# Attention and routed experts on one core: row statistics taken one batch ahead, and the order of the hand-over changed

## The chip, the cores and the metric

One core of a Trainium2 chip runs the whole program. The metric is device time in microseconds (us), lower is better. A run is one execution; the kernel before has three plain ones and one that was profiled.

## The reference

The input `x` is 8 batches of 512 rows of 512 values. Cut to what matters:

```python
xn = (x - mean(x)) / sqrt(var(x) + 1e-5)              # per row
qkv = xn @ Wqkv.T + b_qkv                             # 16 heads of 32
p = softmax(q @ k.T / sqrt(32) + alibi_bias, causal)
s = (p @ v).reshape(...) @ Wout.T + b_out
top_idx = argmax(softmax(xn @ w_router.T))            # 2 experts
h = xn @ w_fc[top].T; a = where(h >= 0, h, 0.5 * h) ** 2
g = silu((a @ w_proj[top].T) * top_weight)
out = x + s * g
```

## The kernel before

The core's engines run programs of their own, written out by hand, each in its own order, and wait for one another on semaphores: TensorE (PE), VectorE (DVE), ScalarE (ACT), GpSimd (POOL), and SyncE (SP), which issues most DMAs.

**Attention** runs batch by batch. `batches` calls each engine's `iteration(b, odd)` for b from -1 to 8; an iteration has 16 steps, one for each head. In one step TensorE transposes the probabilities of this head (L446, `ptrans`), works one or two jobs of the table `JOBS`, and makes the scores of the head four steps ahead (L425, `scores`). The jobs of a step are in `STEP`:

```python
JOBS = [("q", 0, 2), ("ctx", -1, 3), ("k", 0, 2), ("q", 0, 3), ("k", 0, 3),
        ("o", -1, 0), ("x", 1, 0), ("ctx", 0, 0), ("o", -1, 1), ("x", 1, 1),
        ("x", 1, 2), ("o", -1, 2), ("o", -1, 3), ("x", 1, 3),
        ("q", 1, 0), ("ctx", 0, 1), ("logits", 1, 0), ("k", 1, 0), ("q", 1, 1),
        ("k", 1, 1), ("v", 1, 0), ("ctx", 0, 2), ("rank", 1, 0), ("v", 1, 1),
        ("v", 1, 2), ("v", 1, 3)]
STEP = [(0, 1), (2,), (3,), (4,), (5, 6, 7), (8, 9), (10, 11), (12, 13),
        (14, 15), (16, 17), (18,), (19,), (20, 21), (23, 22), (24,), (25,)]
```

The second entry of a job is the batch it belongs to, counted from b, and the third its part. So steps 0 to 3 make the last q and k of batch b, steps 4 to 7 its predecessor's output projection and the transposes of xn for batch b+1, steps 8 to 15 q, k, router logits, v and ranks of batch b+1. "ctx" (L461, `pv`) is the product of probabilities and v for four heads.

VectorE works through one step in this order: `rden` (L868, the reciprocal of the softmax sums of the next head); four masked row minima (L857, `masked`) for the head three steps ahead; `read_out` of the step's job, which for q and k is the cast to 16 bits L782 of what ScalarE has staged (L519); the copy of a third of the transposes (L844, `turned`); then what the step has besides. That is, before the change: `ln_stats` (L749, L750: mean and variance of the rows of batch b+1) twice each in steps 0 and 1, `ln_apply` (L756) in steps 2 to 5, the largest weight (L888) in four steps, and the cast `cx` of a finished context (L900).

TensorE's last score of a step waits for the fourth `masked` of that step (`ttr_done`). Its transposes in step n+1 wait for GpSimd's normalisation `pr` (L941, four instructions) that GpSimd runs in step n, after `rden`. GpSimd also makes the low halves `pre` (L947) and `cx` (L961), the reciprocal deviations `veps` and `rstd` (L953, L956) in step 1, and the indirect DMAs that write each row's routing record (`route`, L969) in steps 14 and 15. `choose` (L784, in step 9) picks the expert from the logits, `place` (L802, in step 13) works out where each row goes.

**Hand-over and experts.** In the last attention batch (b = 7) and in iteration 8 the program finds the scales of the expert weights (`weight_row`, `weight_scales`), splits the first six pieces of them into two 16-bit halves (`split_hi` on ScalarE L1163, `split_lo` on VectorE L1225), and transposes the first rows of the experts (`xtrans` L1080, `turn_hi` L1174, `turn_lo` L1249). Iteration 8 also reads out the last context (L528, L900, L961), for which the last output projection waits (L352, x48). Then come 17 slots of 256 rows through the experts (L1106, L1126).

## Time and profile before

| | |
|---|---|
| median of three runs | 1480.56 us (1479.88 to 1480.98) |
| the profiled execution, its own time | 1481.51 us |
| its span, first to last instruction | 1479.7 us |
| mean granted TensorE clock | 0.987 of full speed |
| busy share of the span: PE, DVE, ACT, POOL | 94%, 62%, 52%, 46% |
| one full attention batch (of which six run alike) | about 85.4 us |
| start of the expert part | about 755.5 us |

The span and the time of a run differ by 1.8 us, which lies outside the first and the last instruction. Step 0 of the batch looked at most starts at 235.1 us and the next batch at 320.6 us. In the timelines below, the first number is the start in us from the span's start, the second how long the entry took (x4: four instructions together), and brackets at the end give how long the engine had stood idle just before and what ended that. A busy time of TensorE counts overlapping matmuls, so its gaps are better read from starts.

### The profile page before, as it was taken

The numbers are of one execution on the slowest core, as the hardware profiler recorded it, in microseconds if no ns is written. First come the engines' busy times: TensorE is split into PE (matmuls) and PEld (weight loads), VectorE is DVE, ScalarE is ACT, GpSimd is POOL, SyncE is SP. The second block draws the span as 40 slices with busy tenths as digits, with TensorE's granted clock in tenths as the row PEclk, the third lists the DMA queues.
The fourth block names the chain that finished last, engine by engine and source line by source line (L and its number), as shares of the span: only waits on it lengthen the run. The fifth ranks groups of instructions, "written<-read, shape, count | busy, mean of one in ns | idle before, by whom it ended". The sixth has DMA issues, their size and how long they took to land.

```text
span 1479.7 us, 30039 instructions
## 1 busy us (share of the span) xinstructions
PE 1384.0 (94%) x9863; PEld 880.8 (60%) x9863; DVE 923.9 (62%) x2441; ACT 770.7 (52%) x1824; POOL 682.5 (46%) x896
## 2 busy tenths in 40 slices
PE   2889999999999999999689999999999999999995
PEld 1455555655555565555456666666666666666663
DVE  7577777777777777777759745555444555544444
ACT  3478778787777878787736422222222222222221
POOL 0356667465666746566523433333333333323332
...
GB/s 161 144 86 148 125 115 125 110 139 100 171 101 130 128 106 138 89 141 140 107 164 207 115 44 44 44 43 25 23 41 42 39 44 44 30 29 30 36 30 30
DMA packets 84897, 133.45 MB, mean 90 GB/s; under 512 B 14095, under 2 KB 63247, under 8 KB 82576
## 3 DMA queue, kind: packets, MB, share of 16 engines
...
## 4 chain that ended last, share of the span: by engine, by line
PE 75%; DVE 10%; POOL 6%; ACT 3%; issue 3%; DMA 1%; DVEq 1%; SPq 0%; ACTq 0%; POOLq 0%
PE psY L1126 19%; PE psF L1106 19%; PE psA L352 19%; PE psT L446 7%; PE psA L461 5%; POOL pr L941 4%; PE psS L425 3%; DVE sg L1303 2%; PE psX L1080 1%; POOL route L969 1%; PE psA L409 1%; DVE stat L749 1%; DVE am L636 1%; ACT stage L519 1%; DVE wf L1225 1%
## 5 line engine op out<-in xcount | busy, mean ns | idle before, releaser
L1106 PE MATMUL psF<-xT,wf 128*128 128x256 f16 (+1 forms) x3264 | 368.0, 269 | 0.0
L1126 PE MATMUL psY<-wf,aT 128*128 x1584 | 363.9, 379 | 0.3 <-DVE aT L1270 0.3
L1106 PEld LDWEIGHTS psF<-xT,wf 128*128 x3264 | 312.0, 98 | 63.5
L1344 POOL TENSOR_TENSOR a<-a 128x512 f32<-128x512 f32 (+1 forms) x136 | 153.1, 1126 | 392.1 <-DVE a L1261 390.5
L941 POOL TENSOR_SCALAR pr<-pr,rden 128x128 f32<-128x128 f32 (+3 forms) x512 | 268.4, 542 | 141.9 <-DVE rden L868 140.3
L579 ACT ACTIVATE pr<-pr,mn 128x128 f32<-128x128 f32 (+3 forms) x512 | 281.9, 553 | 0.0
L857 DVE CUSTOM_DVE_ANT_0 pr<-psS,base,nsl 128x128 f32<-128x128 f32 (+3 forms) x512 | 249.6, 543 | 4.2 <-PE psS L425 4.2
L1126 PEld LDWEIGHTS psY<-wf,aT 128*128 128x128 f16 x1584 | 154.5, 98 | 158.5 <-issue 1.0
L446 PE MATMUL psT<-conf,pr 128*128 128x128 f32 x1280 | 205.7, 279 | 18.1 <-POOL pr L941 16.5
L1183 ACT ACTIVATE rl<-psF 128x512 f32<-128x512 f32 (+1 forms) x136 | 79.3, 583 | 263.2 <-PE psF L1106 263.0
L446 PEld LDWEIGHTS psT<-conf,pr 128*128 128x128 f32 x1280 | 157.3, 143 | 81.3 <-POOL pr L941 27.3
L1190 ACT ACTIVATE aT<-a 128x512 f16<-128x512 f32 (+1 forms) x136 | 84.0, 618 | 230.9 <-POOL a L1344 230.9
L352 PE MATMUL psA<-xT,wqkv 128*128 128x512 f16 x768 | 188.8, 386 | 14.4 <-DVE wqkv L667 13.1
L1261 DVE SCALAR_TENSOR_TENSOR a<-psF,rl 128x512 f32<-128x512 f32 (+1 forms) x136 | 91.7, 674 | 169.4 <-ACT rl L1183 168.5
L566 ACT ACTIVATE pt<-psT 128x512 f32<-128x512 f32 x256 | 151.6, 593 | 62.0 <-PE psT L446 56.2
L1270 DVE TENSOR_TENSOR aT<-a,aT 128x512 f16<-128x512 f32 (+1 forms) x136 | 91.3, 672 | 128.9 <-ACT aT L1190 116.1
L352 PEld LDWEIGHTS psA<-xT,wqkv 128*128 128x128 f16 x768 | 74.9, 99 | 83.8 <-DVE wqkv L667 13.5
L947 POOL TENSOR_TENSOR pre<-stage,pre 128x512 f16<-128x512 f32 x64 | 74.1, 1158 | 90.3 <-DVE pre L782 90.3
L425 PE MATMUL psS<-ks,qs 128*128 128x128 f16 (+3 forms) x512 | 99.8, 304 | 16.2 <-DVE mn L857 12.7
L352 PE MATMUL psA<-wout,cx 128*128 128x512 f16 x384 | 93.2, 385 | 7.4 <-POOL cx L961 7.4
L579 ACT ACTIVATION_READ_ACCUMULATOR pr<-pr,mn 128x1 f32 x512 | 98.3, 192 | 0.0
L782 DVE CAST pre<-stage 128x512 f16<-128x512 f32 x64 | 34.1, 532 | 100.4 <-ACT stage L519 97.8
...
## 6 DMA issues: line engine op xcount, KB each, us to landing
...
qs<-qk_parts SPq DMA_DIRECT2D x128, 128.0 KB, 2.7
ks<-qk_parts SPq DMA_DIRECT2D x128, 128.0 KB, 2.7
...
```

What stands on the lines that cost most here:

```text
L352: last = nc.tensor.matmul(ps, a, x, start=(n == 0), stop=(n == len(pairs) - 1))
L425: nc.tensor.matmul(rows[i], qs[:, par, j, i * P:(i + 1) * P], ks[:, par, j, 0:(i + 1) * P], start=True, stop=True).then_inc(s["S_done"], 1)
L446: last = nc.tensor.transpose(ps[:, o:o + P], pr[:, j, c:c + P], conf[:, C_ID:C_ID + P])
L566: nc.scalar.activation(pt[:, g % 2, j, o:o + w], psT[r][:, 0:w], ACT.Copy).then_inc(s["T_act"], 1)
L579: nc.scalar.activation(p_, p_, ACT.Exp, bias=mn[:, c:c + 1], scale=-1.0, accum_out=den[:, c:c + 1]).then_inc(s["exp_done"], 1)
L857: nc.vector.tensor_tensor_reduce(out=pr[:, h % HG, ROWOFF[i]:ROWOFF[i] + w], in0=rows[i], in1=base[:, S - w:S], scale=nsl[:, h:h + 1], sca ...
L941: nc.gpsimd.tensor_scalar(p_, p_, rden[:, c:c + 1], 32768.0, ALU.mult, ALU.mult).then_inc(s["norm_done"], 1)
L1106: last = nc.tensor.matmul(psF[c % 2][:, k * TT:k * TT + tn], w(e, 2 * hc, hl, kc * 512 + col, P), xT[:, r % 2, x, kc, 0:tn], start=(m == 0 ...
L1126: last = nc.tensor.matmul(psY[r % 2][h][:], aT[:, c % 4, x, k, h * P:(h + 1) * P], w(e, 2 * hc + 1, hl, q * 512, 512), start=(c == 0 and k ...
L1261: nc.vector.scalar_tensor_tensor(out=part(a[:, c % 2, :], n), in0=part(psF[c % 2][:], n), scalar=2.0 ** -28, in1=part(rl[:, c % 2, :], n), ...
L1270: tt(aT[:, c % 4, 1, :, 0:tn], part(a[:, c % 2, :], n), aT[:, c % 4, 0, :, 0:tn], ALU.subtract).then_inc(s["U_lo"], 1)
L1344: nc.gpsimd.tensor_tensor(at, at, at, ALU.mult).then_inc(s["a_ready"], 1)
```

## The change

Five things move. The work itself is the same but for the parity in `mv`.

1. **Statistics a batch ahead.** `ln_stats` for batch b+2 runs in steps 9 and 11 of iteration b instead of steps 0 and 1 of the next one; `mv` is double. GpSimd's `veps`/`rstd` move from step 1 to step 12. SyncE loads x of batch b+2 in iteration b, behind `stack(b, 3)`, instead of at the start of iteration b+1. For batch 0 nothing moves.
2. **`choose` and `place` cut up.** Only the read of the logits stays in step 9; the rest goes behind steps 10 and 11. Of `place`, the read of the ranks stays in step 13, and the rest follows behind steps 13 and 14. The four routing DMAs move from steps 14 and 15 to steps 4 to 7 of the next iteration (to steps 4 and 5 in the last batch).
3. **Last group's context halves.** The cast `cx` of the fourth group moves from the end of step 2 to the end of step 1, and GpSimd's half from behind `pre` to ahead of it in step 2.
4. **Hand-over.** In iteration 8 ScalarE reads the last context ahead of the weight pieces 2 to 5, and VectorE casts it ahead of its own; TensorE's second `xtrans` moves behind the context product.
5. **Weight scales a step later**, from step 14 to the end of step 15 of the last batch.

```diff
 WMAX_LAST = (2, 4, 9, 11)
 ROUTE_AT = (1, 3, 5, 6)
+STATS_AT = {9: (0, 1), 11: (2, 3)}
...
-        mv = sb("mv", [P, QB, 2], F32)
+        mv = sb("mv", [P, 2, QB, 2], F32)
...
-            if within(b, 0, B - 1):
-                for i in range(QB):
-                    wait(sp, s["xn_ready"], b * QB + i + 1, s["apart_sp"])
-                    sp.dma_start(xin[:, i, :], io["x"][bass.ds((b + 1) * S + i * P, P), :]
-                                 ).then_inc(x_in[i], 16)
+            if within(b, -1, B - 2):
+                for i in range(QB):
+                    wait(sp, s["xn_ready"], (b + 1) * QB + i + 1)
+                    sp.dma_start(xin[:, i, :], io["x"][(b + 2) * S + i * P:(b + 2) * S + (i + 1) * P, :]
+                                 ).then_inc(x_in[i], 16)
...
-                if b == B - 1 and step == 13:
+                if b == B - 1 and step == 14:
                     pe.wait_ge(s["fam_row"], 1)
                     nc.tensor.matmul(psA[0][:, 0:2], ones2[:], famd[:], start=True, stop=True
                                      ).then_inc(s["fam_spread"], 1)
-                if b == B - 1 and step >= 14:
-                    ffn["xtrans"](pe, 0, step - 14)
+                if (b, step) in ((B - 1, 14), (B, 0)):
+                    ffn["xtrans"](pe, 0, int(b == B))
...
-                if (b, step) in ((B - 1, 15), (B, 0)):
-                    ffn["split_hi"](act, range(2 * (step == 0), 2 * (step == 0) + 2))
-                if b == B and step in (0, 2):
-                    ffn["turn_hi"](act, 0, step // 2, 0)
-                    ffn["split_hi"](act, range(4 + step // 2, 5 + step // 2))
+                if (b, step) == (B - 1, 15):
+                    ffn["split_hi"](act, range(0, 2))
+                if b == B and step < 2:
+                    ffn["turn_hi"](act, 0, step, 0)
+                if (b, step) == (B, 1):
+                    ffn["split_hi"](act, range(2, 6))
...
-            def ln_stats(i):
-                wait(dve, x_in[i], (nxt + 1) * 16)
+                dve.wait_ge(s["dve_link"], n_link[0])
+            def ln_stats(batch, i):
+                wait(dve, x_in[i], (batch + 1) * 16)
                 link(nc.vector.bn_stats(stat[:, i, :], xin[:, i, :]))
...
+            def choose_rest(part):
+                if part == 0:
+                    dve.wait_ge(s["logits_read"], nxt + 1)
+                    link(nc.vector.tensor_tensor(dl[:], lg[:, :, 1], lg[:, :, 0], ALU.subtract))
+                    nc.vector.scalar_tensor_tensor(out=nd[:], in0=dl[:], scalar=-1.0, in1=dl[:],
+                                                   op0=ALU.mult, op1=ALU.min).then_inc(s["nd_ready"], 1)
+                else:
+                    link(ts(ef[:, 0:QB], dl[:], 0.0, None, ALU.is_gt))
...
+                    nc.vector.memset(t0[:, 0:1], 0.0).then_inc(s["e_ready"], 1)
...
+            def place_rest(part):
+                if part == 0:
+                    dve.wait_ge(s["rank_read"], nxt + 1)
+                    nc.vector.tensor_copy(esum[:, 0:1], rk[:, QB:QB + 1])
...
+                    nc.vector.tensor_copy(pos[:], t0[:])
+                else:
+                    nc.vector.tensor_copy(meta[:, :, 0], tid[:])
+                    link(ts(t1[:], ex[:], 1.0, None, ALU.add))
...
+                    link(ts(tid[:], tid[:], float(S), None, ALU.add))
+                    nc.vector.memset(rk[:, 0:1], 0.0).then_inc(s["meta_ready"], 1)
...
-                if more:
-                    if step < 2:
-                        ln_stats(2 * step)
-                        ln_stats(2 * step + 1)
-                    elif step < 6:
-                        ln_apply(step - 2)
+                if b == -1 and step < 2:
+                    ln_stats(0, 2 * step)
+                    ln_stats(0, 2 * step + 1)
+                if more and 2 <= step < 6:
+                    ln_apply(step - 2)
+                if within(b, -1, B - 2):
+                    for i in STATS_AT.get(step, ()):
+                        ln_stats(b + 2, i)
+                if more and step in (10, 11):
+                    choose_rest(step - 10)
+                if more and step in (13, 14):
+                    place_rest(step - 13)
                 at = WMAX_AT if b < B - 1 else WMAX_LAST
                 if within(b, 0, B) and step in at:
...
                     nc.vector.tensor_tensor(fam[:, c:c + 1], fam[:, c:c + 1], fam[:, 2:3], ALU.max
                                             ).then_inc(s["wm_link"], 1)
                     dve.wait_ge(s["wm_link"], b * 4 + m + 1)
-                if j == (3 if g else 2):
+                if j == (3 if g else 1):
                     pb, pg = (b, g - 1) if g else (b - 1, NG - 1)
                     if within(pb, 0, B):
...
                 if b == B - 1 and step == 13:
                     weight_row()
                     ffn["norm"](dve, 0, 0, 0)
-                if b == B - 1 and step == 14:
-                    weight_scales()
                 if b == B - 1 and step == 15:
                     ffn["norm"](dve, 0, 1, 0)
+                    weight_scales()
                     ffn["split_lo"](dve, range(0, 2))
                 if b == B and step == 0:
-                    ffn["split_lo"](dve, range(2, 4))
-                if b == B and step in (1, 3):
-                    ffn["turn_lo"](dve, 0, step // 2, 0)
-                    ffn["split_lo"](dve, range(4 + step // 2, 5 + step // 2))
-            assert not more or k[0] == LINKS, k[0]
+                    ffn["turn_lo"](dve, 0, 0, 0)
+                if b == B and step == 3:
+                    ffn["turn_lo"](dve, 0, 1, 0)
+                    ffn["split_lo"](dve, range(2, 6))
         batches(dve, iteration)
...
+        def ctx_low(batch, group):
+            if within(batch, 0, B):
+                pool.wait_ge(s["ctx_hi"], batch * NG + group + 1)
+                nc.gpsimd.tensor_tensor(cx[:, group, 1, :], cf[:], cx[:, group, 0, :], ALU.subtract
+                                        ).then_inc(s["ctx_lo"], 1)
+        def deviations(batch):
+            pool.wait_ge(s["ln_stats"], (batch + 1) * QB)
+            wait(pool, s["meta_ready"], batch - 1)
+            nc.gpsimd.tensor_scalar(veps[:], mv[:, batch % 2, :, 1], 1e-5, 1.0, ALU.add, ALU.mult
+                                    ).then_inc(s["pool_link"], 1)
+            pool.wait_ge(s["pool_link"], batch + 1)
+            nc.gpsimd.tensor_tensor(rstd[:, batch % 2, :], veps[:], half[:], ALU.pow
+                                    ).then_inc(s["rstd_ready"], 1)
         def iteration(b, odd):
             nxt, par = b + 1, 1 - odd
             more = within(b, -1, B - 1)
...
                         p_ = pr[:, rh % HG, ROWOFF[i]:ROWOFF[i] + (i + 1) * P]
                         nc.gpsimd.tensor_scalar(p_, p_, rden[:, c:c + 1], 32768.0, ALU.mult, ALU.mult
                                                 ).then_inc(s["norm_done"], 1)
+                if step == 2:
+                    ctx_low(b - 1, NG - 1)
                 for kind, bj, i, _, _ in jobs(b, odd, step, ("q", "k")):
                     w = int(kind == "k")
                     wait(pool, s["qk_hi"], (bj * NG + i) * 2 + 1 + w, s["apart_pool"])
                     nc.gpsimd.tensor_tensor(pre[:, w, 1, :], stage[:, w, :], pre[:, w, 0, :],
                                             ALU.subtract).then_inc(s["qk_lo"], 1)
-                if more and step == 1:
-                    wait(pool, s["ln_stats"], (nxt + 1) * QB, s["apart_pool"])
-                    wait(pool, s["meta_ready"], nxt - 1, s["apart_pool"])
-                    nc.gpsimd.tensor_scalar(veps[:], mv[:, :, 1], 1e-5, 1.0, ALU.add, ALU.mult
-                                            ).then_inc(s["pool_link"], 1)
-                    wait(pool, s["pool_link"], nxt + 1, s["apart_pool"])
-                    nc.gpsimd.tensor_tensor(rstd[:, par, :], veps[:], half[:], ALU.pow
-                                            ).then_inc(s["rstd_ready"], 1)
-                pb, pg = (b, g - 1) if g else (b - 1, NG - 1)
-                if j == (3 if g else 2) and within(pb, 0, B):
-                    wait(pool, s["ctx_hi"], pb * NG + pg + 1, s["apart_pool"])
-                    nc.gpsimd.tensor_tensor(cx[:, pg, 1, :], cf[:], cx[:, pg, 0, :], ALU.subtract
-                                            ).then_inc(s["ctx_lo"], 1)
+                if b == -1 and step == 1:
+                    deviations(0)
+                if within(b, -1, B - 2) and step == 12:
+                    deviations(b + 2)
+                if g and j == 3:
+                    ctx_low(b, g - 1)
                 if b == B - 1 and step in (10, 12):
                     ffn["gather_x"](pool, 0, 0, (step // 2 - 5,))
-                if more and step in (14, 15):
-                    wait(pool, s["meta_ready"], nxt + 1, s["apart_pool"])
-                    for i in (2 * step - 28, 2 * step - 27):
+                if within(b, 0, B) and 4 <= step < (6 if b == B - 1 else 8):
+                    pool.wait_ge(s["meta_ready"], b + 1)
+                    for i in ((2 * step - 8, 2 * step - 7) if b == B - 1 else (step - 4,)):
                         nc.gpsimd.indirect_dma_start(
                             out=io["meta"], out_offset=bass.IndirectOffsetOnAxis(ap=pos[:, i:i + 1], axis=0),
                             in_=meta[:, i, :], in_offset=None).then_inc(s["meta_out"], 16)
```

**VectorE, end of step 9 of a full batch.** Before (`lg` to `t` is `choose`, `pre` and `pt` are the job's cast and the transposes' copy, `rden` opens step 10):

```order
L788 TENSOR_SCALAR lg<-psA,sc 128x8 [waits R2_done,R_done]
L791 TENSOR_TENSOR dl<-lg 128x4 [waits logits_read]
L792 SCALAR_TENSOR_TENSOR nd<-dl 128x4 [waits dve_link]
L794 TENSOR_SCALAR ef<-dl 128x4
L795 CAST e<-ef 128x4 [waits dve_link]
L796 CAST epre<-ef 128x1
L798 TENSOR_TENSOR epre<-epre,ef 128x1 [waits dve_link] x3
L800 MEMSET t 128x1 [waits dve_link]
L782 CAST pre<-stage 128x512 [waits k_stored,qk_staged]
L844 COPY pt<-psT 128x256 [waits T_done]
L868 RECIPROCAL rden<-den 128x4 [waits norm_done,exp_done]
```

And now:

```order
L789 TENSOR_SCALAR lg<-psA,sc 128x8 [waits R2_done,R_done]
L783 CAST pre<-stage 128x512 [waits k_stored,qk_staged]
L855 COPY pt<-psT 128x256 [waits T_done]
L750 BN_STATS stat<-xin 128x6 [waits x_in0]
L751 BN_AGGR mv<-stat 128x2 [waits dve_link]
L750 BN_STATS stat<-xin 128x6 [waits x_in1]
L751 BN_AGGR mv<-stat 128x2 [waits dve_link]
L879 RECIPROCAL rden<-den 128x4 [waits norm_done,exp_done]
```

The eight small instructions ahead of the cast have gone, and two pairs of statistics stand between the copy `pt` and the next `rden`.

**VectorE, end of step 11.** Before:

```order
L857 ISA mn 128x1
L782 CAST pre<-stage 128x512 [waits k_stored,qk_staged]
L844 COPY pt<-psT 128x256 [waits T_done]
L900 CAST cx<-cf 128x512 [waits O_done,ctx_staged]
L868 RECIPROCAL rden<-den 128x4 [waits norm_done,exp_done]
```

And now:

```order
L855 COPY pt<-psT 128x256 [waits T_done]
L750 BN_STATS stat<-xin 128x6 [waits x_in2]
L751 BN_AGGR mv<-stat 128x2 [waits dve_link]
L750 BN_STATS stat<-xin 128x6 [waits x_in3]
L751 BN_AGGR mv<-stat 128x2 [waits dve_link]
L800 TENSOR_SCALAR ef<-dl 128x4
L801 CAST e<-ef 128x4 [waits dve_link]
L802 CAST epre<-ef 128x1
L804 TENSOR_TENSOR epre<-epre,ef 128x1 [waits dve_link] x3
L806 MEMSET t 128x1 [waits dve_link]
L917 CAST cx<-cf 128x512 [waits O_done,ctx_staged]
L879 RECIPROCAL rden<-den 128x4 [waits norm_done,exp_done]
```

Ahead of the cast `cx` and of the `rden` of step 12 there are now two more pairs of statistics and the second part of `choose`.

**GpSimd, steps 1 to 3 of a full batch** (`pr` is the normalisation, `pre` the low half of q or k). Before, from the last `pr` of step 1 (cut ahead of step 3's):

```order
L941 TENSOR_SCALAR pr<-pr,rden 128x512
L947 TENSOR_TENSOR pre<-stage,pre 128x512 [waits qk_hi]
L953 TENSOR_SCALAR veps<-mv 128x4 [waits meta_ready,ln_stats]
L956 TENSOR_TENSOR rstd<-veps,half 128x4 [waits pool_link]
L941 TENSOR_SCALAR pr<-pr,rden 128x128 [waits rden_done]
L941 TENSOR_SCALAR pr<-pr,rden 128x256
L941 TENSOR_SCALAR pr<-pr,rden 128x384
L941 TENSOR_SCALAR pr<-pr,rden 128x512
L947 TENSOR_TENSOR pre<-stage,pre 128x512 [waits qk_hi]
L961 TENSOR_TENSOR cx<-cf,cx 128x512 [waits ctx_hi]
```

And now:

```order
L973 TENSOR_SCALAR pr<-pr,rden 128x512
L981 TENSOR_TENSOR pre<-stage,pre 128x512 [waits qk_hi]
L973 TENSOR_SCALAR pr<-pr,rden 128x128 [waits rden_done]
L973 TENSOR_SCALAR pr<-pr,rden 128x256
L973 TENSOR_SCALAR pr<-pr,rden 128x384
L973 TENSOR_SCALAR pr<-pr,rden 128x512
L944 TENSOR_TENSOR cx<-cf,cx 128x512 [waits ctx_hi]
L981 TENSOR_TENSOR pre<-stage,pre 128x512 [waits qk_hi]
```

`veps` and `rstd` no longer stand ahead of step 2's `pr`, and `cx` comes ahead of `pre`.

**ScalarE at the hand-over** (`wf` is one weight piece, `cf` the last context). Before:

```order
L1163 ACTIVATE wf<-wstage,sc 128x1024 [waits V_done,wf_in0,qk_done,scaled]
L1163 ACTIVATE wf<-wstage,sc 128x1024 [waits wf_in1]
L1163 ACTIVATE wf<-wstage,sc 128x1024 [waits wf_in2]
L1163 ACTIVATE wf<-wstage,sc 128x1024 [waits wf_in3]
L1174 ACTIVATE xT<-psX 128x4x128 [waits f_X_done,k_stored,q_stored]
L1163 ACTIVATE wf<-wstage,sc 128x1024 [waits wf_in0]
L528 ACTIVATE cf<-psA,bqs,sc 128x512 [waits ctx_lo,PV_done]
L1174 ACTIVATE xT<-psX 128x4x128 [waits f_X_done]
```

And now:

```order
L1188 ACTIVATE wf<-wstage,sc 128x1024 [waits V_done,wf_in0,qk_done,scaled]
L1188 ACTIVATE wf<-wstage,sc 128x1024 [waits wf_in1]
L1199 ACTIVATE xT<-psX 128x4x128 [waits f_X_done,k_stored,q_stored]
L529 ACTIVATE cf<-psA,bqs,sc 128x512 [waits ctx_lo,PV_done]
L1199 ACTIVATE xT<-psX 128x4x128 [waits f_X_done]
L1188 ACTIVATE wf<-wstage,sc 128x1024 [waits wf_in2]
L1188 ACTIVATE wf<-wstage,sc 128x1024 [waits wf_in3]
```

The read of the context stands behind two weight pieces and one turn, where five pieces and one turn were ahead of it.

## Rows read from the trace of the kernel before

**Rows 1.** Busy time by stretch: a full batch, then the experts. Columns: stretch, length, engines, clock, DMA.

```profile
232.60:318.00 85.40, 82.15 (x612) 49.23 (x611) 63.85 (x226) 66.38 (x182) 52.64 (x83) 1.00 0.41 124
...
800.00:1480.00 680.00, 661.51 (x4655) 447.65 (x4652) 339.67 (x519) 196.27 (x327) 239.92 (x218) 0.99 0.14 43
```

**Rows 2.** Timeline of TensorE in the batch of 235.1 to 320.6 us: start, us, then the row.

```profile
250.74 0.39 PE L425 MATMUL psS<-ks,qs 128*128 128x512 f16 x1 [0.34 <-DVE mn L857]
...
252.94 0.66 PE L446 MATMUL psT<-conf,pr 128*128 128x128 f32 x4 [1.81 <-POOL pr L941]
...
257.22 0.66 PE L446 MATMUL psT<-conf,pr 128*128 128x128 f32 x4
...
295.83 0.60 PE L446 MATMUL psT<-conf,pr 128*128 128x128 f32 x4
...
304.59 2.36 PE L461 MATMUL psA<-pt,v 128*32 128x512 f32 x32
```

**Rows 3.** Timeline of VectorE in the same batch.

```profile
246.31 0.43 DVE L782 CAST pre<-stage 128x512 f16<-128x512 f32 x1 [1.56 <-ACT stage L519]
...
246.98 0.68 DVE L749 BATCH_NORM_STATS2 stat<-xin 128x6 f32<-128x512 f32 x1
...
248.59 0.16 DVE L868 RECIPROCAL rden<-den 128x4 f32<-128x4 f32 x1
...
288.97 0.16 DVE L794 TENSOR_SCALAR ef<-dl 128x4 f32<-128x4 f32 x1
...
290.05 0.06 DVE L800 MEMSET t<- 128x1 f32 x1
...
292.56 0.18 DVE L868 RECIPROCAL rden<-den 128x4 f32<-128x4 f32 x1
...
300.99 1.28 DVE L900 CAST cx<-cf 128x512 f16<-128x512 f32 x1
...
302.19 0.17 DVE L868 RECIPROCAL rden<-den 128x4 f32<-128x4 f32 x1
```

**Rows 4.** Timeline of GpSimd in the same batch.

```profile
246.82 1.16 POOL L947 TENSOR_TENSOR pre<-stage,pre 128x512 f16<-128x512 f32 x1 [1.86 <-DVE pre L782]
...
249.05 1.04 POOL L956 TENSOR_TENSOR rstd<-veps,half 128x4 f32<-128x4 f32 x1
...
250.18 2.70 POOL L941 TENSOR_SCALAR pr<-pr,rden 128x128 f32<-128x128 f32 x4
...
255.12 2.05 POOL L941 TENSOR_SCALAR pr<-pr,rden 128x128 f32<-128x128 f32 x4
...
300.82 1.16 POOL L947 TENSOR_TENSOR pre<-stage,pre 128x512 f16<-128x512 f32 x1 [1.03 <-DVE pre L782]
```

**Rows 5.** Timelines of the hand-over: VectorE, then ScalarE, GpSimd and TensorE.

```profile
731.74 0.42 DVE L900 CAST cx<-cf 128x512 f16<-128x512 f32 x1
...
732.07 0.54 DVE L1243 TENSOR_SCALAR xn<-xg,rec 128x512 f32<-128x512 f32 x1
...
732.90 5.40 DVE L1225 SCALAR_TENSOR_TENSOR wf<-wstage,sc,wf 128x1024 f16<-128x1024 f32 x4 [0.28 <-ACT wf L1163]
...
741.21 0.42 DVE L900 CAST cx<-cf 128x512 f16<-128x512 f32 x1
...
731.71 4.26 ACT L1163 ACTIVATE wf<-wstage,sc 128x1024 f16<-128x1024 f32 x4
...
739.88 0.76 ACT L528 ACTIVATE cf<-psA,bqs,sc 128x512 f32<-128x512 f32 x1
...
741.71 1.15 POOL L961 TENSOR_TENSOR cx<-cf,cx 128x512 f16<-128x512 f32 x1 [8.09 <-DVE cx L900]
...
743.01 12.52 PE L352 MATMUL psA<-wout,cx 128*128 128x512 f16 x48 [7.39 <-POOL cx L961]
```

**Rows 6.** Busy time in batch 0 and at the hand-over, columns as in rows 1.

```profile
92.00:94.00 2.00, 2.00 (x20) 0.87 (x16) 1.95 (x10) 0.00 (x0) 1.81 (x4) 0.50 0.52 142
...
743.00:747.00 4.00, 3.99 (x10) 1.44 (x11) 0.94 (x1) 0.00 (x0) 0.00 (x0) 0.50 0.00 0
```

49 lines of the change are left out of this document (17 added, 32 removed).

## The prediction

> **What bounds the kernel now.** I read the busy time by stretch first. In a full batch of 85.4 us TensorE is busy 82.15 us, and in the experts' 680 us it is busy 661.51 us [rows 1]; VectorE (63.85), ScalarE (66.38) and GpSimd (52.64) have 19 us and more free. So TensorE bounds, and every term below is time in which it waits, or begins to wait. The experts' part has the same instructions in the same order; the change can move its start alone.
>
> The timelines come next, because a sum of busy time does not show whether an instruction is on the path. TensorE's last score of step 2 waits 0.34 us for VectorE's masked minimum, and its transposes of step 3 wait 1.81 us for `pr` [rows 2]. To the left of that wait lie three things. On VectorE, `ln_stats` runs from 246.98 to the `rden` at 248.59, so 1.61 us for two blocks [rows 3]. On GpSimd, `rstd` ends at 250.09, so `pr` can start only at 250.18, and it takes 2.70 us; then come `pre`, `cx` and the next `pr` at 255.12, and step 4's transposes start at 257.22, just as that `pr` (2.05 us) ends [rows 2, 4]. Steps 2 to 4 thus hang on GpSimd.
>
> There is a measure that I use throughout. The last score of a step starts 2.1 us behind that step's `rden`, when VectorE is the late one: 248.59 to 250.74, and 302.19 to the context product at 304.59, ahead of which stands such a score [rows 2, 3]. When nothing is late, TensorE gets there a little later than VectorE lets it; in step 3 (nothing besides) I find about 1 us of such room. Whatever VectorE does behind the copy `pt` and ahead of `rden` beyond that room delays TensorE one for one. What it does ahead of the cast `pre` costs nothing, since there it waits for ScalarE anyway (1.56 us idle at 246.31 [rows 3]).
>
> **Part 1 and 3, steps 1 to 4: a gain.** Without statistics the `rden` of step 2 could start at 246.98, but the cast `cx` now stands there. GpSimd begins `pre` at 246.82 for 1.16 us [rows 4], and a cast that begins beside such a `pre` takes not 0.43 but 1.28 us (300.99 beside 300.82), the next instruction starting 1.20 us behind it [rows 3, 4]. So `rden` at 246.98 + 1.20 = 248.18, against 248.59; the last score at 250.3; `pr` at 248.45 (`rden` takes 0.16, and a hop some 0.1), since `veps` and `rstd` are gone, to 250.50. Step 3 begins at about 250.55 instead of 252.94: 2.4 us less. That gain is not all kept, because GpSimd is the late one next: `pr` to 250.50, `cx` 1.16, `pre` 1.16, `pr` 2.05 make 254.87, and VectorE's cast and `ln_apply` fall beside them. One collision of 0.8 us (1.28 less 0.43) puts step 4 at 255.7 against 257.22: **-1.5 us a batch**. The bounds are 254.87 (no collision, -2.35) and -0.9 (`pr` takes 2.70 again). In iteration 0 there is no earlier context, so `cx` is absent on GpSimd too and about half of the chain's surplus with it: I take -2.25 there.
>
> **Part 1, step 9: a loss.** The statistics (1.61 us) now stand behind `pt`, ahead of the `rden` that starts at 292.56 [rows 3]. `choose` leaves the place ahead of the cast, where it was covered by the wait for ScalarE, and frees nothing. `rden` at 294.17, the last score at 296.32, and step 11's transposes 0.2 us behind that, 296.53 against 295.83 [rows 2]: **+0.7 us**. The room of this step has taken 0.9 of the 1.6.
>
> **Parts 1 and 2, step 11: the largest term.** Before, the cast `cx` was alone between `pt` and `rden` and cost 1.20 us (300.99 to 302.19). Now there come 1.61 us of statistics, the second part of `choose`, 288.97 to about 290.1, so 1.12 us, and then the cast, which `pre` (to 301.98 [rows 4]) no longer touches. Such a cast, undisturbed, lets the next instruction start 0.33 us on (731.74 to 732.07 [rows 5]). Together 3.06 us, so 1.86 more. The context product followed its last score at once (304.59), so there is no room: **+1.86 us**. Its bounds are +0.7 (if the first block is taken by room that I don't see) and +2.7 (the cast collides as well).
>
> **Parts 2 and small moves.** The first part of `choose` in step 10 and of `place` in step 13 are two to seven instructions of 0.06 to 0.16 us each [rows 3], in steps with 1 us of room; `place`'s second part in step 14 is about 0.9 us at that price and takes the room whole; the routing DMAs leave GpSimd's steps 14 and 15. Together +0.1 us. The four DMAs in steps 4 to 7 stand behind `pr` and `pre`, where GpSimd waits for the next `rden`; step 7's is ahead of step 8's `cx`-free `pr`, and I cost them at nothing, because GpSimd has 33 us free in the batch [rows 1]; if the cover fails, each costs up to 1 us. The Trainium skill, same page, section "Who interferes with whom", would have such a DMA's descriptors blocked while VectorE runs a two-port operation; by that rule the four would each end later, and no run here shows a price yet. SyncE's four loads of x are now issued some 40 us ahead of their use in step 9, behind `stack(b, 3)`; what they hold up is the queue of weight loads and stores behind them, which is not waited for in a batch. `veps` and `rstd` in step 12 (1.3 us) follow that step's `pr` and end before the next one. In iteration 7 there is nothing but the earlier `cx`: 0. Ahead of batch 0, in iteration -1, the statistics of batch 1 join steps 9 and 11 and `place` is cut up, where few heads' work stands beside them: 0.
>
> **Part 4 and 5, hand-over: a gain.** Now ScalarE takes four pieces from 731.71 (4.26 us, 1.07 each), a turn and a fifth piece before `cf` at 739.88; VectorE takes four (5.40 us, 1.35 each) from 732.90, and casts at 741.21; GpSimd adds 1.15, and the output projection starts at 743.01 after 7.39 us idle [rows 5]. The scales now stand behind `norm` (732.07, 0.54), so they, six small instructions that start 0.2 us apart (as `choose`'s do [rows 3]), are ready at 732.6 + 1.3 = 733.9. ScalarE: 733.9 + 2 x 1.07 + a turn of 0.6 (an estimate: a read of as many values as `cf`'s 0.76) + `cf` 0.76 = 737.4. VectorE: first low half at 735.0, two of 1.35 make 737.7, the turn 0.6, the cast 0.35: 738.65. GpSimd 1.15 and a hop of 0.1: 739.9, against 743.01: **-3.1 us**. Pieces 2 to 5 are split while the output projection runs (12.52 us [rows 5]), with 4 x 1.35 = 5.4 us needed. If that cover were gone it would cost up to 3 us.
>
> **Sum.** Iterations 1 to 5 each -1.5 + 0.7 + 1.86 + 0.1 = +1.16, together +5.8. Iteration 0: -2.25 + 2.56 + 0.1 = +0.4. Iteration 6 has no statistics, so step 11 gains only `choose`: -1.5 + (1.12 + 0.33 - 1.20) + 0.1 = -1.1. Hand-over -3.1. In all +2.0 us. On the profiled execution's own 1481.51 us (span 1479.7) that is 1483.5; on the median of 1480.56, which is 0.95 lower, 1482.6.
>
> **Rivals.**
> (a) *The statistics find room in steps 9 to 12.* Then the +2.56 of six iterations goes, in all -15.4: 1467.2; with half of it hidden 1474.9. For it: VectorE is busy only 63.85 of 85.4 us [rows 1]. Against: its free time lies ahead of the casts, not behind `pt`. It decides if the room of step 11 is above 2 us.
> (b) *The clock.* The granted clock is 0.50 (the 1.2 GHz level) in 92 to 94 us and again in 743 to 747 us with TensorE fully busy, the latter right behind the 7.39 us of idling [rows 5, 6]. If the shorter idling (4.3 us) no longer leads to the lower level, those 4 us of work take 2, and the same in batch 0 takes another 2: 1478.6. The Trainium skill, page TensorE: Matmul & The Clock Gate, Part 1, says that idling throttles the array; the trace agrees.
> (c) *Slower: one more collision a batch.* The later `cx` and the later minima of step 12 fall beside GpSimd's `pr`. At 0.85 us in each of six iterations +5.1: 1487.7. It decides when the cast begins less than 1.1 us behind a GpSimd instruction.
> (d) *The hand-over gives nothing*, since VectorE's low halves start late and the output projection still waits: +3.1, 1485.7.
>
> **How the numbers follow.** Chances: forecast 0.42, (a) at least in part 0.17, (b) 0.14, (c) 0.15, (d) 0.12. The forecast's own range, from the bounds of -1.5 and +1.86, is 1478 to 1486. To hold 8 in 10 I go down into (a) and up to (c): 1475 to 1488. A measurement of this kernel tells about 0.2%, or 3 us, from no change. Faster: nearly all of (a), half of (b), a little of the forecast, 0.25. Slower: (c), (d) and the forecast's upper third, 0.36. The same: 0.39.
>
> **What would show it.** In the profile after: step 3's wait for `pr` (1.81) gone, and step 4's transposes 1 to 2 us earlier against step 0; `rstd` in step 12; a new wait for VectorE's minimum at the last score of step 10 (about 0.6) and of step 12 (about 2), in iterations 0 to 5 and not in 6; full batches of 86.6 instead of 85.4 us; the output projection waiting about 4 us. The prediction is wrong if the waits of steps 10 and 12 are missing, or if the low clock in batch 0 or at the hand-over goes.

## The result, and the profile after

The changed kernel takes 1487.08 us (median of five, 1485.78 to 1487.68), the kernel before 1480.56: a ratio of 1.0043 with a 95% interval of 1.0028 to 1.0057. It is slower by 0.43%, beyond the 0.2% that can be told apart. The forecast was 1482.6 in a range of 1475 to 1488. The profiled execution took 1487.08 us in all, its span is 1485.3 us, 5.6 more than before.

The same stretches by busy time, and three short windows for the clock (columns as in [rows 1]):

```profile
232.60:318.00 85.40, 81.77 (x593) 47.98 (x592) 63.77 (x215) 63.81 (x174) 52.03 (x82) 0.98 0.41 124
...
800.00:1480.00 680.00, 667.05 (x4694) 451.42 (x4691) 344.58 (x524) 199.38 (x331) 241.46 (x219) 1.00 0.15 45
...
92.00:94.00 2.00, 1.82 (x17) 1.50 (x16) 0.00 (x0) 2.00 (x7) 0.50 (x1) 1.00 0.50 119
...
88.00:92.00 4.00, 4.00 (x35) 1.66 (x28) 2.69 (x11) 0.34 (x1) 3.78 (x6) 0.57 0.38 117
...
308.00:310.00 2.00, 2.00 (x21) 0.87 (x16) 1.78 (x8) 0.00 (x0) 1.90 (x4) 0.50 0.50 132
```

The last of these windows in the kernel before, at full speed:

```profile
308.00:310.00 2.00, 2.00 (x12) 1.15 (x11) 0.00 (x0) 1.35 (x6) 0.23 (x1) 1.00 0.02 6
```

The clock of 92 to 94 us is now 1.00, but the low stretch of iteration 0 has not gone: it lies at 88 to 92 us (0.57 on average), beside the same context product, which now starts at 87.73 instead of 91.00 us and takes 3.88 instead of 3.83:

```profile
87.73 3.88 PE L462 MATMUL psA<-pt,v 128*32 128x512 f32 x32
```

New is the low clock (0.50) at 308 to 310 us. TensorE's timeline in the batch that now starts at 235.79 us (0.68 later than before), which answers to [rows 2]:

```profile
251.24 0.66 PE L447 MATMUL psT<-conf,pr 128*128 128x128 f32 x4
...
256.13 0.39 PE L426 MATMUL psS<-ks,qs 128*128 128x512 f16 x1 [0.33 <-DVE mn L868]
...
256.42 0.66 PE L447 MATMUL psT<-conf,pr 128*128 128x128 f32 x4
...
295.48 0.39 PE L426 MATMUL psS<-ks,qs 128*128 128x512 f16 x1 [0.33 <-DVE mn L868]
...
295.71 0.65 PE L447 MATMUL psT<-conf,pr 128*128 128x128 f32 x4
...
306.38 4.05 PE L462 MATMUL psA<-pt,v 128*32 128x512 f32 x32
```

Step 3's transposes (251.24) no longer wait for `pr`. Counted from the batch's start they come 2.38 us earlier than in [rows 2]. Step 4's (256.42) come only 1.49 earlier, because the last score ahead of them (256.13) waits for VectorE. The transposes at 295.71 have a wait of 0.33 ahead of them that was not there. The context product at 306.38 takes 4.05 us instead of 2.36: the low clock. The same place one batch on, undisturbed:

```profile
393.31 0.79 PE L426 MATMUL psS<-ks,qs 128*128 128x128 f16 x3 [1.11 <-DVE mn L868]
...
394.43 0.39 PE L426 MATMUL psS<-ks,qs 128*128 128x512 f16 x1 [0.34 <-DVE mn L868]
...
394.75 2.36 PE L462 MATMUL psA<-pt,v 128*32 128x512 f32 x32
```

The two waits ahead of the context product are 1.11 and 0.34 us. VectorE's timeline in the first of these batches, for [rows 3]:

```profile
247.67 1.28 DVE L917 CAST cx<-cf 128x512 f16<-128x512 f32 x1
...
248.87 0.17 DVE L879 RECIPROCAL rden<-den 128x4 f32<-128x4 f32 x1
...
251.21 1.39 DVE L783 CAST pre<-stage 128x512 f16<-128x512 f32 x1 [0.32 <-ACT stage L520]
...
252.86 1.27 DVE L757 TENSOR_SCALAR xn<-xin,mv,rstd 128x512 f32<-128x512 f32 x1
...
293.33 0.16 DVE L879 RECIPROCAL rden<-den 128x4 f32<-128x4 f32 x1
...
300.92 0.68 DVE L750 BATCH_NORM_STATS2 stat<-xin 128x6 f32<-128x512 f32 x1
...
302.53 0.14 DVE L800 TENSOR_SCALAR ef<-dl 128x4 f32<-128x4 f32 x1
...
303.63 0.43 DVE L917 CAST cx<-cf 128x512 f16<-128x512 f32 x1
...
303.97 0.17 DVE L879 RECIPROCAL rden<-den 128x4 f32<-128x4 f32 x1
```

And GpSimd's, for [rows 4]:

```profile
247.50 1.16 POOL L981 TENSOR_TENSOR pre<-stage,pre 128x512 f16<-128x512 f32 x1 [3.46 <-DVE pre L783]
...
249.13 2.06 POOL L973 TENSOR_SCALAR pr<-pr,rden 128x128 f32<-128x128 f32 x4 [0.47 <-DVE rden L879]
...
251.15 1.17 POOL L944 TENSOR_TENSOR cx<-cf,cx 128x512 f16<-128x512 f32 x1
...
252.68 1.16 POOL L981 TENSOR_TENSOR pre<-stage,pre 128x512 f16<-128x512 f32 x1 [0.36 <-DVE pre L783]
...
254.31 2.06 POOL L973 TENSOR_SCALAR pr<-pr,rden 128x128 f32<-128x128 f32 x4 [0.47 <-DVE rden L879]
...
307.70 1.04 POOL L954 TENSOR_TENSOR rstd<-veps,half 128x4 f32<-128x4 f32 x1
```

`pr` follows `rden` at 249.13, at once; `rstd` is away in step 12 (307.70). The cast `cx` (247.67) took 1.28 us beside GpSimd's `pre` (247.50), as forecast. From the first statistics block at 300.92 to `rden` at 303.97 are 3.05 us (forecast 3.06), with the undisturbed cast (0.43) at their end. At the hand-over, TensorE, ScalarE, VectorE and GpSimd in turn, for [rows 5]:

```profile
740.30 4.05 PE L462 MATMUL psA<-pt,v 128*32 128x512 f32 x32 [0.61 <-ACT pt L567]
...
748.57 13.19 PE L353 MATMUL psA<-wout,cx 128*128 128x512 f16 x48 [3.62 <-POOL cx L944]
...
761.60 2.67 PE L1131 MATMUL psF<-xT,wf 128*128 128x256 f16 x23
```

```profile
742.59 2.19 ACT L1188 ACTIVATE wf<-wstage,sc 128x1024 f16<-128x1024 f32 x2 [2.43 <-DVE sc L734]
...
745.17 0.77 ACT L529 ACTIVATE cf<-psA,bqs,sc 128x512 f32<-128x512 f32 x1
```

```profile
740.41 0.54 DVE L1268 TENSOR_SCALAR xn<-xg,rec 128x512 f32<-128x512 f32 x1
...
741.25 0.73 DVE L731 TENSOR_SCALAR sc<-sc 128x2 f32<-128x2 f32 x1
...
746.77 0.41 DVE L917 CAST cx<-cf 128x512 f16<-128x512 f32 x1
```

```profile
747.27 1.16 POOL L944 TENSOR_TENSOR cx<-cf,cx 128x512 f16<-128x512 f32 x1 [5.31 <-DVE cx L917]
```

TensorE waits 3.62 us for the last context (7.39 before); 1.7 us of the difference is only that the product ahead of the wait took 4.05 instead of 2.36 us, and in changed_again, where it took 2.36, the wait is 5.33. The gain is therefore better read from VectorE: from its `norm` (L1268 now, L1243 before) to the output projection are 8.16 us, against 10.94 in [rows 5].

### The profile page after: what moved, and what is told of

Its sections match the earlier page's. It is cut to its first block, busy times and chain, and to the rows that moved or that the text cites. A ratio compares the mean times of both kernels' runs of the same rounds, so it can differ in the third digit from the quotient of the medians.

```text
span 1485.3 us, 30039 instructions
## 1 busy us (share of the span) xinstructions
PE 1394.9 (94%) x9863; PEld 882.4 (59%) x9863; DVE 938.3 (63%) x2441; ACT 772.2 (52%) x1824; POOL 682.3 (46%) x896
## 4 chain that ended last, share of the span: by engine, by line
PE 74%; DVE 15%; issue 4%; ACT 4%; POOL 2%; DMA 1%; DVEq 1%; SPq 0%; POOLq 0%
PE psF L1131 20%; PE psY L1151 19%; PE psA L353 18%; PE psT L447 7%; PE psA L462 5%; PE psS L426 3%; DVE pr L868 3%; DVE sg L1328 2%; ACT stage L520 1%; PE psX L1105 1%; DVE stat L750 1%; PE psA L410 1%; POOL pr L973 1%; DVE pt L855 1%; DVE fam L905 1%
## 5 line engine op out<-in xcount | busy, mean ns | idle before, releaser
L973 POOL TENSOR_SCALAR pr<-pr,rden 128x128 f32<-128x128 f32 (+3 forms) x512 | 265.1, 536 | 146.3 <-DVE rden L879 145.0
L426 PE MATMUL psS<-ks,qs 128*128 128x128 f16 (+3 forms) x512 | 106.0, 306 | 29.9 <-DVE mn L868 25.1
L783 DVE CAST pre<-stage 128x512 f16<-128x512 f32 x64 | 37.9, 592 | 93.7 <-ACT stage L520 93.7
```

Of the source, the lines that this page charges most:

```text
L426: nc.tensor.matmul(rows[i], qs[:, par, j, i * P:(i + 1) * P], ks[:, par, j, 0:(i + 1) * P], start=True, stop=True).then_inc(s["S_done"], 1)
L973: nc.gpsimd.tensor_scalar(p_, p_, rden[:, c:c + 1], 32768.0, ALU.mult, ALU.mult).then_inc(s["norm_done"], 1)
```

## Where the 5.6 us come from

All kernels make TensorE's steps in the same order, so I took the start of each step's first transposes in both traces, and subtracted lengths. The full batch of before from 320.58 to 406.04 us is the undisturbed example; its numbers repeat within 0.03 us in the others unless said. Below, each kernel against before, in us, by step:

```
                step 2  step 3  step 6  step 10 step 11 step 12  whole batch
changed         -2.38   +0.89   +0.02   +0.69   +0.05   +1.86    +1.22
dev_back        -1.13   +0.15   +0.02   +0.69   +0.05   +1.85    +1.71
ctx_only        -0.15    0.00   +0.01   -0.01    0.00    0.00    -0.10
ctx_back        -2.66   +2.02   +0.01   +0.69   +0.04   +1.86    +2.05
choose_whole    -2.38   +0.88   +0.01   +0.68   +0.05   +0.73    +0.06
stats_in_gap    -2.39   +0.89   +0.01    0.00   +0.23   +1.31    +0.12
all_gap         -2.66   +0.21   +0.01   -0.01   +0.01   -0.01    -2.35
all_gap_apply   -2.65   -0.06   -0.43    0.00    0.00    0.00    -3.09
room_one        -2.66   -0.06   -0.44   -0.01   +0.01   +0.06    -3.07
all_cx_gap      -2.65   -0.07   -0.44   -0.01   +0.01   -0.22    -3.35
```

(Step 2 is the time from its first transposes to those of step 3, and so on, so a late `rden` of step 3 shows in the column of step 3. The rest of the batch differs by at most 0.1 in sum.)

For the changed kernel, iteration by iteration: ahead of batch 0 -0.55; iteration 0 +0.01; 1, 3 and 4 +1.22 each; 2 +2.91, of which 1.7 is the one product at the low clock; 5 +1.41; 6 -0.26; 7 -0.16; from the last step (718.76, now 725.78) to the experts' first product (755.36, now 761.60) -0.78; the rest -0.64. Together +5.6.

## The experiments

Each ran beside the kernel before on its chip, whose medians were 1480.4 to 1481.0 us.

**Statistics where VectorE waits (stats_in_gap).** One block each in steps 8 to 11, ahead of the jobs' `read_out`:

```diff
-STATS_AT = {9: (0, 1), 11: (2, 3)}
+STATS_AT = {8: (0,), 9: (1,), 10: (2,), 11: (3,)}
...
+                if within(b, -1, B - 2):
+                    for i in STATS_AT.get(step, ()):
+                        ln_stats(b + 2, i)
                 for args in jobs(b, odd, step, ("q", "k", "x", "o", "logits", "rank")):
                     read_out(*args)
                 turned(2)
...
-                if within(b, -1, B - 2):
-                    for i in STATS_AT.get(step, ()):
-                        ln_stats(b + 2, i)
```

> The changed kernel (1487.08 us), but the four blocks of statistics stand one each in steps 8 to 11, ahead of the job's cast, where VectorE waits for ScalarE; choose stays cut up. Theory (what stands behind the copy pt and ahead of rden delays TensorE one for one beyond about 1 us of room, what stands ahead of the cast costs nothing): the +0.70 of step 10 goes, and step 12 keeps only choose's second part (as in iteration 6 of the changed kernel, +0.90 against before instead of +1.86), in all about -10 us, 1477. Rival 1 (the statistics cost their 3.2 us wherever they stand): 1487. Rival 2 (choose's second part is the whole cost): 1487 less at most 1.

Measured: 1477.41 us (1474.85 to 1478.1), ratio 0.9977 (0.9967 to 0.9986). The +0.69 of step 10 is gone; step 12 kept +1.31, where I expected +0.9. VectorE in iteration 2, and its cast of the same step in iteration 6, which has no statistics; then GpSimd in iteration 2:

```profile
295.32 0.69 DVE L750 BATCH_NORM_STATS2 stat<-xin 128x6 f32<-128x512 f32 x1
...
296.14 0.41 DVE L783 CAST pre<-stage 128x512 f16<-128x512 f32 x1
...
296.80 1.02 DVE L800 TENSOR_SCALAR ef<-dl 128x4 f32<-128x4 f32 x1
...
298.78 0.43 DVE L917 CAST cx<-cf 128x512 f16<-128x512 f32 x1
...
299.12 0.17 DVE L879 RECIPROCAL rden<-den 128x4 f32<-128x4 f32 x1
...
638.24 0.43 DVE L783 CAST pre<-stage 128x512 f16<-128x512 f32 x1 [0.31 <-ACT stage L520]
```

```profile
296.63 1.16 POOL L981 TENSOR_TENSOR pre<-stage,pre 128x512 f16<-128x512 f32 x1 [1.01 <-DVE pre L783]
```

The missing 0.4 is the block of statistics in step 11. The place ahead of the cast is free only as long as VectorE idles there. In iteration 6 it idles 0.31 us (638.24), because `choose`'s first part has made it late in step 10; the block needs 0.80, so the cast at 296.14 comes without any idling and about 0.5 us late. With `choose` whole (all_gap, below) that idling is 0.61 us even behind the block, and step 12 loses nothing. The +0.9 itself is `choose`'s second part: a comparison of four values a row, which takes 0.14 us in the changed kernel (302.53), took 1.02 at 296.80, just behind GpSimd's `pre` at 296.63. It now stands directly behind `pt`, where `cx` had collided before. Both rivals fall: in steps 8 to 10 the same work costs nothing ahead of the cast, and `choose` was only part of the cost. That the time met the expected 1477 is in part luck: an undisturbed batch is 1.10 us shorter than the changed kernel's, where 1.66 were expected, and the two profiles differ besides by 1.7 us of low clock in iteration 2, by 3.05 us in iteration 0 (half of it its first context product, 2.36 instead of 3.88 us behind the same waits) and by 1.6 us at the hand-over, which the edit does not touch.

**`choose` whole again (choose_whole).** `choose_rest(0)` and `(1)` right behind `choose` in step 9, the calls in steps 10 and 11 gone.

> The changed kernel with choose back in one piece in step 9, ahead of the cast, as before the change; statistics stay behind pt. Theory: step 10 still +0.70, step 12 has 1.61 + 0.33 instead of 3.06 us between pt and rden, so +0.74 instead of +1.86 against before: -1.1 in six iterations and -0.9 in iteration 6, about -7.6 us, 1479.5. Rival (the statistics alone fill the room, cutting choose up is free): 1487.

Measured: 1475.9 us (1472.99 to 1476.94), ratio 0.9966 (0.9953 to 0.9978). Step 12 keeps +0.73 against an expected +0.74, and iteration 6 is 1.42 us shorter than before instead of 0.26. In the two profiles that is 1.1 to 1.2 us for an iteration, 8.0 in seven. The median came out 3.6 us lower than expected; of that the profiles show 1.7 as iteration 2's product, which ran at full clock here, behind a shorter wait (see changed_again below), and 1.3 ahead of batch 0, which nothing shown ties to the edit.

**GpSimd's deviations back in step 1 (dev_back).**

```diff
-                if within(b, -1, B - 2) and step == 12:
-                    deviations(b + 2)
+                if within(b, 0, B - 1) and step == 1:
+                    deviations(b + 1)
```

> The changed kernel with GpSimd's veps and rstd back at the end of step 1; the statistics they read are still made an iteration ahead. Theory (the wait of 1.81 us for pr in step 3 hung on GpSimd's rstd more than on VectorE's statistics): pr of step 2 starts about 1.0 us later than in the changed kernel, step 3's transposes 1.0 later, step 4's about the same 1.0, in iterations 0 to 6: +6 to +7 us, 1493. Rival (the gain came from taking the statistics off VectorE, and GpSimd has room): 1487.

Measured: 1490.4 us (1487.34 to 1492.91), ratio 1.0059 (1.0042 to 1.0076). GpSimd:

```profile
253.16 1.04 POOL L954 TENSOR_TENSOR rstd<-veps,half 128x4 f32<-128x4 f32 x1
...
254.30 2.21 POOL L973 TENSOR_SCALAR pr<-pr,rden 128x128 f32<-128x128 f32 x4
...
258.90 2.05 POOL L973 TENSOR_SCALAR pr<-pr,rden 128x128 f32<-128x128 f32 x4
```

`pr` of step 2 waits for `rstd` again (it would start 1.1 us earlier), and step 3 begins 1.25 us later than in the changed kernel. But step 4 is only 0.5 later: in the changed kernel the next `pr` had waited for VectorE's `rden` (0.47 us idle at 254.31, and 0.36 ahead of `pre`), and that slack took 0.7 of it. So +0.5 a batch, not +1.0, and the median lies 3.3 us above the changed kernel's instead of 6 to 7: the wait was right, its size was not.

**The cast `cx` alone, and undone (ctx_only, ctx_back).** The first is the kernel before with part 3, the second the changed kernel without it.

> The kernel before with part 3 alone (cast cx at the end of step 1, GpSimd's half ahead of pre in step 2); statistics and rstd stay in steps 0 and 1. Theory: the rden of step 2 is 1.2 us later, but pr still waits for rstd, so steps 3 and 4 stay where they are: 1480.5, within 1 us. Rival (moving cx made the gain of steps 2 to 4): 1470.

> The changed kernel with part 3 undone (cast cx at the end of step 2, GpSimd's half behind pre). Theory: step 3 begins up to 0.6 us earlier, since rden of step 2 no longer waits for the cast, and step 4 as late as before or later, since the cast and ln_apply both stand ahead of its rden: within 2 us of 1487. Rival (part 3 carried the gain): 1493 or more.

Measured: ctx_only 1478.7 us (1475.75 to 1481.01), ratio 0.9983 (0.9974 to 0.9993), ctx_back 1494.27 us (1492.78 to 1498.63), ratio 1.0097 (1.0079 to 1.0115). ctx_only lies 1.8 us below the expected 1480.5, outside the 1 us given. Of its 2.3 us less, the full batches give 0.10 each, as expected; 1.96 lie in iteration 0, where before the granted clock was 0.50 in 92 to 94 us and here 1.00. The first context product took 2.36 us there, behind the same waits as before (1.40 and 0.33 us); whether part 3 has a hand in that is not shown. For ctx_back I was wrong. With part 3 undone a batch costs 0.83 us more (in the columns of step 2 and 3, -0.28 and +1.12), 5 to 6 us in all:

```profile
253.08 0.42 DVE L917 CAST cx<-cf 128x512 f16<-128x512 f32 x1
...
253.41 0.17 DVE L879 RECIPROCAL rden<-den 128x4 f32<-128x4 f32 x1
```

The cast stands behind a 1.27 us `ln_apply` and holds up the `rden` of step 3 at 253.41, GpSimd's `cx` then comes ahead of `pr`, and that `pr` took 2.49 us. The rest of the 7 us goes with the low clock, which step 12 has in three iterations of that profile against one of the changed kernel's, and step 4 of iteration 5 besides (1.7 us); how much of the medians' difference it makes is not shown. Part 3 is thus worth 0.1 us a batch while `rstd` is late and 0.8 once it is not.

**The hand-over alone (hand_only).** The kernel before with parts 4 and 5.

> The kernel before (1480.56 us) with parts 4 and 5 alone: the context ahead of weight pieces 2 to 5, the scales a step later. Theory: the output projection starts 3.1 us earlier against the last context product at full clock; where the clock falls to its lower level beside the context product (4.05 instead of 2.36 us in the changed kernel) only 1.5: 1477.5 to 1479.0. Rival (it gives nothing, the shorter idling is lost elsewhere): 1480.5.

Measured: 1477.83 us (median of 12, 1476.06 to 1481.5), ratio 0.998 (0.9971 to 0.9989): 3.0 us less, the size that was forecast. The executions fall into two groups, nine at 1476.06 to 1478.61 and three at 1481.15 to 1481.5 with mean clocks of 0.984 to 0.986 (0.986 to 0.989 in the nine); the profiled one (1481.15) is of the second, so its trace shows no gain in all. But from `norm` to the output projection it has 8.18 us, as the changed kernel (8.16) and changed_again (8.17), against 10.94 before. I had worked out 7.8. What was missing stands in the changed kernel's row at 741.25: one of the six small instructions took 0.73 instead of 0.17 us, behind GpSimd's half of the previous context (at 740.58, 1.38 us).

**The changed kernel again (changed_again).**

> The changed kernel once more, for a second profile. Theory (in step 12 TensorE now idles 1.1 and 0.33 us just ahead of the context product, and sometimes, not always, the granted clock then falls to 0.50 for the product's 4 us): 1487, with the step that was 1.7 us longer in one iteration of six now in another iteration, or in none or two. Rival (the fall belongs to that place in the program): the same iteration again.

Measured: 1485.76 us (median of 8, 1482.06 to 1488.81), ratio 1.003 (1.0019 to 1.0041). This profile has three context products of step 12 near 4 us, in iterations 2, 4 and 5, against one, in iteration 2. One row of iteration 2:

```profile
306.46 3.86 PE L462 MATMUL psA<-pt,v 128*32 128x512 f32 x32
```

Neither theory nor rival is quite right: the iteration recurred, and two more came. By kernel, the number of step 12 products in iterations 1 to 6 that ran at the low clock in the profile: in the four with +1.86 in step 12 (changed, changed_again, dev_back, ctx_back) 1, 3, 3 and 3 of six; in the nine others (before among them) none of 54. In iteration 6 the wait of 1.1 us is not there, so these are 10 of the 20 products behind it; in iteration 0, with the same waits, it was none of four. One more place bears this out: the first context product of iteration 0 stands behind waits of 1.1 to 1.4 and 0.3 us in ten of the thirteen kernels, before among them, and ran at the low clock in seven of the ten; in the three where the first wait is 0.52 (all_gap_apply, room_one, all_cx_gap) it ran at full clock. What decides in which execution and iteration it comes stays open. The two executions of this kernel with the highest mean clock (0.988) took 1482.06 and 1483.53 us, the one with the lowest (0.983) 1488.81.

**Everything in the gap (all_gap, all_gap_apply).** Statistics as in stats_in_gap, `choose` whole, `cx` of the fourth group ahead of step 1's job on VectorE and ahead of `pre` in step 1 on GpSimd; in the second also `ln_apply` ahead of `read_out`. VectorE's part, without what is as in the runs above:

```diff
+                if step == 1:
+                    ctx_high(b - 1, NG - 1)
+                if more and 2 <= step < 6:
+                    ln_apply(step - 2)
                 for args in jobs(b, odd, step, ("q", "k", "x", "o", "logits", "rank")):
                     read_out(*args)
...
-                if more and 2 <= step < 6:
-                    ln_apply(step - 2)
```

> The changed kernel with everything movable put ahead of the job's cast, where VectorE waits for ScalarE: statistics one block each in steps 8 to 11, choose whole in step 9, the cast cx of the fourth group ahead of step 1's job, and GpSimd's half of it ahead of step 1's pre. Theory: against before nothing is lost in steps 10 and 12, step 3 is 2.4 us earlier in each iteration and the 0.9 that the changed kernel gave back in step 4 is not given back, since cx no longer stands between GpSimd's pr of step 2 and of step 3: -2.3 us in seven iterations, -0.5 ahead of batch 0, -1.5 to -3 at the hand-over, so 1461 to 1463. Rival (what is put ahead of the cast delays the cast itself or GpSimd's pre, and q and k come late): above 1470.

> all_gap with ln_apply too ahead of the job in steps 2 to 5 instead of behind pt. Theory: its 0.54 to 1.27 us (the long ones beside GpSimd) leave the path of steps 2 to 5; where TensorE does not wait for them it gives nothing: 0 to -2 us against all_gap. Rival (they now delay the job's own read, the output projection's and the transposes' in steps 4 and 5): +1 to +5 us.

Measured: 1458.77 us (1458.33 to 1460.53), ratio 0.9855 (0.984 to 0.987), and 1453.42 us (1451.29 to 1453.79), ratio 0.9813 (0.9799 to 0.9826). A batch is 2.35 and 3.09 us shorter than before. The first came out 2 us below its 1461 to 1463: the batches are as expected, but iteration 0 gave 4.6 us instead of 2.3, 1.5 of that its first context product at full clock (2.36 instead of 3.83 us). The second gave 5.4 us where I expected at most 2: besides 0.27 in step 3 it removed a loss of 0.43 in step 6 of every batch, which I had not looked at, and 0.84 in iteration 0.

**How much room (room_one).** Of all_gap_apply, the blocks of steps 9 and 10 back behind `pt`, one in each.

> all_gap_apply (1453.42 us) with two of the four blocks of statistics put back behind pt, but one each, in steps 9 and 10, where nothing else stands. Theory (a step has 0.9 us of room between pt and rden, and one block is 0.80): no change, 1453.4 within 1 us; two blocks in one step cost 0.70 in the changed kernel. Rival (whatever stands behind pt costs its whole time): 0.8 us twice in seven iterations, +11, 1464.

Measured: 1453.05 us (1450.15 to 1454.12), ratio 0.9807 (0.9793 to 0.9821): no change. One block of 0.80 us fits, two cost 0.69. The room is about 0.9 us in such a step.

**The other casts too (all_cx_gap).** `ctx_high(b, g - 1)` and `ctx_low(b, g - 1)` ahead of the jobs in steps 7, 11 and 15.

> all_gap_apply with the casts cx of the other three groups also ahead of the job's cast (steps 7, 11, 15), and GpSimd's halves ahead of its pre. Theory: the cast that took 1.28 us beside GpSimd's pre in step 11 leaves the path, 0.2 to 0.4 us in each of seven or eight iterations, 1450.5 to 1453. Rival (in step 11 one block of statistics, this cast and its collision no longer fit ahead of the job's cast, and q or k is late): +1 us or more in each, 1460.

Measured: 1448.66 us (1446.47 to 1450.0), ratio 0.9782 (0.9769 to 0.9796), the fastest: 2.2% less than before, and below the expected 1450.5 to 1453. A batch gains 0.25 us, in step 12. VectorE in step 11:

```profile
369.21 0.60 DVE L890 CAST cx<-cf 128x512 f16<-128x512 f32 x1
...
369.72 0.67 DVE L750 BATCH_NORM_STATS2 stat<-xin 128x6 f32<-128x512 f32 x1
...
370.72 1.05 DVE L785 CAST pre<-stage 128x512 f16<-128x512 f32 x1
...
372.02 0.16 DVE L881 RECIPROCAL rden<-den 128x4 f32<-128x4 f32 x1
```

All of it, the cast `pre` (1.05 us now) included, stands ahead of a `rden` that comes early enough. The median gained 4.8 us where batches explain some 1.7; in this profile the hand-over was 2.7 us shorter than in all_gap_apply's (31.99 against 34.69 us from the last step to the experts). Of that 0.9 is the edit's: from context product to output projection 7.37 us instead of 8.28, 0.6 since the previous context's half on GpSimd no longer blocks a scale, and 0.3 since its cast no longer stands ahead of `norm`. And 1.35 is the output projection itself (11.85 against 13.20 us), the same instructions at another clock.

## Why the prediction was right or wrong

The time lay within the range, 4.5 us above the forecast and on the slower side, which had 0.36 against 0.39 for no change. The forecast change was +2.0 us and the measured one 6.5, so the range held by its width more than by the sum: several terms were off, most of them upwards. The forecast's own range, 1478 to 1486, is also narrower than the bounds it was said to come from: over six iterations the bounds of -1.5 and +1.86 alone reach from 12 us below to 9 us above.

- **Step 10, +0.7, and step 12, +1.86.** Right to 0.02 us, in every undisturbed batch. The rule behind them (what stands between `pt` and `rden` beyond the room of the step, 0.9 us in step 9, costs TensorE one for one) is borne out by choose_whole and room_one. Its other half, that work ahead of the cast costs nothing, holds in all_gap; stats_in_gap bounds it by the time that VectorE idles there. Rival (a) falls.
- **Steps 2 to 4, -1.5.** Right (-1.49), on the way that was given in part: step 3 gained 2.38, and a collision of 0.8 us gave 0.89 back. But there were two collisions, not one (the job's cast 1.39 and `ln_apply` 1.27), and VectorE's `rden`, not GpSimd's queue, was last: GpSimd idles 0.36 and 0.47 us. The sum hit by luck, because both ways end near the same time; dev_back's +0.5 instead of +1.0 shows the difference.
- **A full batch, 86.6 us.** It is 86.68.
- **Small moves, +0.1.** In sum they cost 0.1 to 0.2 (+0.05 in step 11, +0.12 in step 15), but not as priced: `choose`'s first part in step 10 begins behind GpSimd's `pre` (296.18 behind 296.01), and its first instruction took 1.01 us instead of 0.16. The room of that step hid it.
- **Iteration 6, -1.1.** It was -0.26. The term there was 1.12 + 0.33 - 1.20 = +0.25 in step 11 for `choose` and the cast; steps 11 and 12 measured +0.24 and +0.90. I had removed the cast's collision from the sum, but where no statistics stand ahead of it, `choose`'s comparison takes the collision over, so +0.25 becomes +1.1. VectorE, then GpSimd, in iteration 6 of the changed kernel:

```profile
648.78 1.02 DVE L800 TENSOR_SCALAR ef<-dl 128x4 f32<-128x4 f32 x1
...
648.62 1.16 POOL L981 TENSOR_TENSOR pre<-stage,pre 128x512 f16<-128x512 f32 x1 [0.59 <-DVE pre L783]
```

- **Iteration 0, +0.4, and ahead of it, 0.** +0.01 and -0.55.
- **Hand-over, -3.1.** The chain was as given, and its term nearly so: from `norm` to the output projection -2.78 us, short of -3.1 by the one blocked instruction. hand_only's median shows 3.0. In the changed kernel's profile the stretch gave 0.78 only, because what lies on both sides was slower: from the last step to `norm` 14.63 against 13.31 us (a context product of 3.33 us at 728.10 is in it), and the output projection 13.03 against 12.35. In changed_again these are 13.80 and 12.10 us, and the whole stretch gave 2.53, so this goes with the clock of an execution, not with the order. The product of 4.05 us at 740.30 costs nothing, since `cf` waits for the scales.
- **The clock.** Rival (b) had it as a gain in batch 0 and at the hand-over; neither was found (0.57 in 88 to 92 us, and 0.50 in 749 to 753 us behind the 3.62 us of idling). It turned out a loss elsewhere: where TensorE now waits in step 12, the context product of some iterations runs at 0.50 of full speed, 1.7 us each, and I had priced a wait at its own length alone. The Trainium skill, page TensorE: Matmul & The Clock Gate, Part 1, has idling as what throttles the array; the row at 306.38, behind such waits, agrees, and the row at 394.75, behind the same waits at full clock, shows that they do not always do it.
- **Rival (c)**, one more collision a batch, ends at nearly the measured time, but step 12 is +1.86 with the cast undisturbed; (d) is refuted by hand_only.

The measured 5.6 us are the 2.0 forecast, + 2.2 in iterations 1 to 5 (1.7 of it the clock), + 0.8 in iteration 6, + 2.3 at the hand-over, less 1.7 in the rest (ahead of batch 0 0.55, iterations 0 and 7 0.55, experts 0.64).
